# Attention in a layernorm, mixture-of-experts and latent-attention block: the causal mask added on VectorE, one reciprocal per head, one context copy on ScalarE

## The reference, cut to what matters

```python
latents = x @ W_down.T                          # (2, 512, 64)
q, k, v = heads(x @ W_q.T), heads(latents @ W_uk.T), heads(latents @ W_uv.T)
scores = q @ k.T / sqrt(128)
scores = where(causal, scores, -inf)            # a query sees the keys up to itself
attn = softmax(scores, axis=-1)
return (attn @ v) @ W_o.T
```

## Time and profile before

| | |
|---|---|
| time, median of 3 runs | 241.64 us (241.52 to 241.77) |
| the profiled execution | 241.79 us, of which the span of the profile is 240.0 us |
| granted TensorE clock | 1.0 of full speed |
| busy: TensorE / weight loads / VectorE / ScalarE / GpSimd | 97% / 73% / 84% / 69% / 36% |
| instructions | 7215, of which VectorE 480 and ScalarE 320 |
| attention, from the first scores to the end of the last context | 57.0 to 188.8 us of the span |

### The profile page before, as it was taken

How to read it: one execution, slowest core, us unless ns; L and a number is a source line. 1 busy time by engine, 2 the same in 40 slices (tenths; PEclk the granted TensorE clock), 3 DMA queues, 4 the chain that set the end, 5 groups by cost and what they waited for, 6 DMA issues and landing times.

```text
span 240.0 us, 7215 instructions
## 1 busy us (share of the span) xinstructions
PE 232.4 (97%) x2620; PEld 175.4 (73%) x2620; DVE 201.8 (84%) x480; ACT 165.2 (69%) x320; POOL 85.6 (36%) x140
## 2 busy tenths in 40 slices
PE   8799999998999999999999999999999999999995
PEld 2455469846679788787887786887888888864474
DVE  3988789988899999899899999998999547368793
ACT  2667873885788889879798888887988400354660
POOL 8342775090024344345334343543255000300320
PEclk9999999999999999999999999999999999999999
DMA  6999963003021034142160250241504240000005
GB/s 214 242 384 330 203 154 87 4 0 87 3 55 38 3 77 98 32 99 44 44 131 0 66 109 21 73 83 44 116 15 90 44 46 0 3 0 3 0 1 175
DMA packets 43128, 19.30 MB, mean 80 GB/s; under 512 B 33820, under 2 KB 42856, under 8 KB 42856
## 3 DMA queue, kind: packets, MB, share of 16 engines
q1 hardware_dynamic: 41912, 17.91, 31.5%
q10 hardware_dynamic: 1200, 1.18, 1.5%
HBM read 7.55 MB, written 1.05 MB: 36 GB/s over the span
## 4 chain that ended last, share of the span: by engine, by line
PE 81%; DVE 9%; ACT 5%; DMA 2%; issue 1%; SPq 1%; DVEq 0%
PE bank L1172 15%; PE bank L981 12%; PE bank L1253 9%; PE bank L932 8%; PE bank L1162 7%; PE bank L1163 7%; PE bank L1185 4%; PE bank L1186 4%; PE bank L1187 4%; PE bank L1089 3%; PE bank L1164 3%; DMA X<-in_L_attn_x_dram 2%; DVE X L765 1%; PE bank L939 1%; DVE st L656 1%
## 5 line engine op out<-in xcount | busy, mean ns | idle before, releaser
L574 ACT ACTIVATE prob<-bank,nmax 128x384 f32<-128x384 f32 (+3 forms) x128 | 62.3, 527 | 10.8 <-DVE nmax L823 7.6
L832 DVE TENSOR_TENSOR pT_lo<-bank,pT_hi 128x512 f16<-128x512 f32 x80 | 54.7, 683 | 2.6 <-ACT pT_hi L580 1.8
L580 ACT CAST pT_hi<-bank 128x512 f16<-128x512 f32 x80 | 46.8, 586 | 10.2 <-PE bank L1172 9.8
L1172 PE MATMUL bank<-ident,prob 128*128 128x128 f32 x320 | 50.5, 280 | 0.6 <-ACT prob L574 0.6
L430 POOL TENSOR_TENSOR cst<-craw,rsum 128x256 f32<-128x256 f32 x30 | 18.4, 614 | 70.7 <-DVE craw L841 70.7
L1162 PE MATMUL bank<-latT_hi,wqo 128*128 128x384 bf16 (+3 forms) x128 | 38.2, 299 | 0.5 <-DMA wqo<-stage 0.5
L1185 PE MATMUL bank<-lat,pT_hi 128*128 128x65 bf16 x320 | 37.7, 193 | 0.3 <-DVE pT_lo L832 0.3
L1186 PE MATMUL bank<-lat,pT_hi 128*128 128x64 bf16 x320 | 37.9, 195 | 0.0
L1187 PE MATMUL bank<-lat,pT_lo 128*128 128x65 bf16 x320 | 37.5, 192 | 0.0
L1163 PE MATMUL bank<-latT_lo,wqo 128*128 128x384 bf16 (+3 forms) x128 | 36.6, 299 | 0.0
L823 DVE TENSOR_REDUCE nmax<-bank 128x1 f32<-128x512 f32 (+1 forms) x48 | 32.7, 682 | 1.9 <-PE bank L1164 1.9
(11 more groups left out here) (179 smaller groups left out, 466.2 us busy)
## 6 DMA issues: line engine op xcount, KB each, us to landing
wqo<-stage SPq DMA_DIRECT2D x64, 64.0 KB, 2.0
wqo<-in_L_attn_W_o_dram SPq DMA_DIRECT2D x2, 1024.0 KB, 6.5
wqo<-in_L_attn_W_q_dram SPq DMA_DIRECT2D x1, 2048.0 KB, 14.0
out_dram<-X SPq DMA_DIRECT2D x8, 128.0 KB, 1.8
X<-in_L_attn_x_dram ACTq DMA_DIRECT2D x1, 512.0 KB, 7.0
cT<-in_L_attn_W_uk_dram SPq DMA_DIRECT2D x1, 512.0 KB, 15.7
cT<-in_L_attn_W_uv_dram SPq DMA_DIRECT2D x1, 512.0 KB, 11.2
cT<-in_L_ffn_w_dram SPq DMA_DIRECT2D x1, 384.0 KB, 4.9
```

The source lines that it names most:

```text
L574: last = nc.scalar.activation(prob[:, u % 2, cols], bank[SCORE_BANK[u]][:, cols], ACT.Exp, bias=nmax[:, u, n:n + 1])
L580: nc.scalar.copy(pT_hi[:, j % 2, :], bank[3 + j % 2][:, :]).then_inc(pThi_ready, 1)
L832: nc.vector.tensor_tensor(pT_lo[:, j % 2, :], bank[3 + j % 2][:, :], pT_hi[:, j % 2, :], ALU.subtract).then_inc(pTlo_ready, 1)
L1172: last = nc.tensor.transpose(bank[3 + j % 2][:, blk(k)], prob[:, j % 2, blk(k)], ident[:, :])
```

## The change

- **Mask.** The matmul of line 1164 goes. `maskneg` grows from 128 to 512 columns, zero but for the triangle in the last 128. `row_max` becomes one `tensor_tensor_reduce` per piece: it adds the end of `maskneg` that is as wide as the piece to the scores, multiplies by -1, writes the negated masked scores back to their place in PSUM, and takes their minimum into `nmax`. The exponential then reads the scores with a scale of -1. `row_max` also waits for the constants.
- **Contexts and sums.** The copies into `craw` take the column of sums along (4x65 in place of 4x64). VectorE still copies the first sequence's contexts; the second sequence's are copied by ScalarE in a new `take_second_context`, between its exponentials and its split in steps 5 and 10. VectorE's new `invert_sums`, at the end of its own steps 5 and 10, waits for both copies and inverts all eight sums of a head out of SBUF in one instruction. GpSimd's division of either sequence waits for that. The last head of the last pair is handled as before.
- **Loop.** VectorE's loop over the pairs is written out in the program.

```diff
--- before.py
+++ after.py
@@ -56,6 +56,7 @@
     SCALE = 1.0 / float(P) ** 0.5
     EPS = 1e-5
     HUGE = 1.5e38
+    FAR = 3.4e38
 
 
     HEAD_UNITS = [[(0, 2, 0), (0, 0, 3 * P)], [(0, 3, 0)], [(0, 1, 0), (1, 1, 2 * P)],
@@ -90,7 +91,7 @@
         identb = sb("identb", [P, P], BF16)
         tri = sb("tri", [P, P], BF16)
         onesb = sb("onesb", [P, P], BF16)
-        maskneg = sb("maskneg", [P, P], BF16)
+        maskneg = sb("maskneg", [P, SB * P], BF16)
         rank_i = sb("rank_i", [P, NB, E], I32)
         rank = sb("rank", [P, NB, E], F32)
         sel = sb("sel", [P, FC, P], BF16)
@@ -181,7 +182,7 @@
         pT_lo = sb("pT_lo", [P, 2, SEQ], FP16)
         nmax = sb("nmax", [P, UNITS, 2], F32)
         rsum = sb("rsum", [P, B, SB], F32)
-        craw = sb("craw", [P, B, SB, LAT], F32)
+        craw = sb("craw", [P, B, SB, LAT + 1], F32)
         cst = sb("cst", [P, B, SB, LAT], F32)
 
         bank = [ctx.enter_context(nc.psum_tensor(f"bank{i}", [P, 512], F32)) for i in range(8)]
@@ -356,7 +357,7 @@
                                     base=0, pattern=[[-1, P]], channel_multiplier=1)
             nc.gpsimd.affine_select(out=tri[:, :], in_=tri[:, :], compare_op=ALU.is_ge, fill=0.0,
                                     base=0, pattern=[[1, P]], channel_multiplier=-1)
-            nc.gpsimd.affine_select(out=maskneg[:, :], in_=maskneg[:, :], compare_op=ALU.is_ge, fill=-1e30,
+            nc.gpsimd.affine_select(out=maskneg[:, SEQ - P:SEQ], in_=maskneg[:, SEQ - P:SEQ], compare_op=ALU.is_ge, fill=-1e30,
                                     base=0, pattern=[[-1, P]], channel_multiplier=1)
             nc.gpsimd.tensor_copy(rank[:, :, :], rank_i[:, :, :])
             nc.gpsimd.affine_select(out=sel[:, :, :], in_=sel[:, :, :], compare_op=ALU.not_equal, fill=1.0,
@@ -427,7 +428,7 @@
                     of_head = slice(LAT * side, LAT * (side + 1))
                     pool.wait_ge(rsum_ready, i * (2 * B) + (side * B + b + 1))
                     pool.wait_ge(ctx_free, i * (2 * B) + (side * B + B + b + 1))
-                    nc.gpsimd.tensor_tensor(cst[:, b, :, :], craw[:, b, :, :],
+                    nc.gpsimd.tensor_tensor(cst[:, b, :, :], craw[:, b, :, 0:LAT],
                                             rsum[:, b, :].unsqueeze(2).to_broadcast([P, SB, LAT]), ALU.mult).then_inc(cst_ready, 1)
                     pool.wait_ge(cst_ready, i * (2 * B) + (side * B + b + 1))
                     hi, lo = (c[:, bass.ds(i, 1), SB * b:SB * (b + 1), of_head].rearrange("p i n l -> p (i n) l") for c in (c_hi, c_lo))
@@ -572,16 +573,26 @@
                 for n, (b, q, at) in enumerate(HEAD_UNITS[u % HU]):
                     cols = slice(at, at + P * (q + 1))
                     last = nc.scalar.activation(prob[:, u % 2, cols], bank[SCORE_BANK[u]][:, cols], ACT.Exp,
-                                                bias=nmax[:, u, n:n + 1])
+                                                bias=nmax[:, u, n:n + 1], scale=-1.0)
                 last.then_inc(prob_ready, 1)
 
             def split(i, j):
                 act.wait_ge(pT_ps, i * UNITS + (j + 1))
                 nc.scalar.copy(pT_hi[:, j % 2, :], bank[3 + j % 2][:, :]).then_inc(pThi_ready, 1)
 
+            def take_second_context(i, side):
+
+                src = bank[6][:, 0:SB * (LAT + 1)].rearrange("p (q l) -> p q l", q=SB)
+                act.wait_ge(clo_ready, i * (2 * B) + (side * B + B))
+                act.wait_ge(ctx_ps, i * (2 * B) + (side * B + B))
+                nc.scalar.copy(craw[:, 1, :, :], src).then_inc(ctx_free, 1)
+
             def attention_step(i, j, queries=True):
+                side, unit = divmod(j - 1, HU)
                 if not beyond(i, j + 3):
                     exponent(i, j + 3)
+                if j and unit == LAST_UNIT[1]:
+                    take_second_context(i, side)
                 if queries and j in (1, 3):
                     split_queries(i + 1, j // 2)
                 if not beyond(i, j + 2):
@@ -816,15 +827,15 @@
 
             def row_max(i, j):
                 u = j % UNITS
+                dve.wait_ge(const_step, 2)
                 dve.wait_ge(s_ps, i * UNITS + (j + 1))
                 parts = HEAD_UNITS[u % HU]
                 src = bank[SCORE_BANK[u]]
-                if len({q for _, q, _ in parts}) == 1:
-                    last = nc.vector.tensor_reduce(nmax[:, u, 0:len(parts)], src[:, :].rearrange("p (a n) -> p a n", a=len(parts)),
-                                                   AX.X, ALU.max, negate=True)
-                else:
-                    for n, (b, q, at) in enumerate(parts):
-                        last = nc.vector.tensor_reduce(nmax[:, u, n:n + 1], src[:, at:at + P * (q + 1)], AX.X, ALU.max, negate=True)
+                for n, (b, q, at) in enumerate(parts):
+
+                    last = nc.vector.tensor_tensor_reduce(
+                        out=src[:, at:at + P * (q + 1)], in0=src[:, at:at + P * (q + 1)], in1=maskneg[:, SEQ - P * (q + 1):SEQ],
+                        scale=-1.0, scalar=FAR, op0=ALU.add, op1=ALU.min, accum_out=nmax[:, u, n:n + 1])
                 last.then_inc(max_ready, 1)
 
             def split(i, j):
@@ -837,8 +848,12 @@
                 src = bank[5 + b][:, 0:SB * (LAT + 1)].rearrange("p (q l) -> p q l", q=SB)
                 dve.wait_ge(clo_ready, i * (2 * B) + (side * B + 1 + b))
                 dve.wait_ge(ctx_ps, i * (2 * B) + (side * B + b + 1))
-                nc.vector.reciprocal(rsum[:, b, :], src[:, :, LAT]).then_inc(rsum_ready, 1)
-                nc.vector.tensor_copy(craw[:, b, :, :], src[:, :, 0:LAT]).then_inc(ctx_free, 1)
+                nc.vector.tensor_copy(craw[:, b, :, :], src).then_inc(ctx_free, 1)
+
+            def invert_sums(i, side):
+
+                dve.wait_ge(ctx_free, i * (2 * B) + (side * B + 2 * B))
+                nc.vector.reciprocal(rsum[:, :, :], craw[:, :, :, LAT]).then_inc(rsum_ready, B)
 
             def normalise_last(b):
 
@@ -852,14 +867,16 @@
 
             def attention_step(i, j, queries=True):
                 side, unit = divmod(j - 1, HU)
-                if j and unit in LAST_UNIT:
-                    take_context(i, side, LAST_UNIT.index(unit))
+                if j and unit == LAST_UNIT[0]:
+                    take_context(i, side, 0)
                 if not beyond(i, j + 1):
                     split(i, j + 1)
                 if not beyond(i, j + 4):
                     row_max(i, j + 4)
                 if queries and j in (1, 3):
                     split_queries(i + 1, j // 2)
+                if j and unit == LAST_UNIT[-1]:
+                    invert_sums(i, side)
 
             def split_latents(t):
                 dve.wait_ge(lat_hi, t + 1)
@@ -886,7 +903,8 @@
             split(0, 0)
             row_max(0, 3)
             attention_step(0, 0)
-            with dve.Fori(0, NP - 1) as i:
+
+            for i in range(NP - 1):
                 for j in range(1, UNITS + 1):
                     attention_step(i, j)
             for j in range(1, UNITS - 2):
@@ -1160,8 +1178,7 @@
                     keys = slice(SEQ * b, SEQ * b + P * (q + 1))
                     queries_of = uc[:, i * 2 + j // HU, SEQ * b + P * q:SEQ * b + P * (q + 1)]
                     mm(dst[:, cols], queries_of, latT_hi[:, keys], start=True, stop=False)
-                    mm(dst[:, cols], queries_of, latT_lo[:, keys], start=False, stop=False)
-                    last = mm(dst[:, cols][:, P * q:], identb[:, :], maskneg[:, :], start=False, stop=True)
+                    last = mm(dst[:, cols], queries_of, latT_lo[:, keys], start=False, stop=True)
                 last.then_inc(s_ps, 1)
 
             def transposes(i, j):
```

## The result

| | before | after |
|---|---|---|
| median | 241.62 us (4 runs) | 243.38 us (4 runs) |
| ratio | | 1.0065, 95% interval 1.0042 to 1.0087 |
| span of the profiled execution | 240.0 us | 241.6 us |
| one trip of the loop (100.50 to 116.80 after) | 16.22 us | 16.30 us |
| end of the last context | 188.8 us | 190.4 us |

Behind the last context both kernels take the same time (240.0 - 188.8 and 241.6 - 190.4, both 51.2). The 1.6 us are lost in attention, and I place them by where TensorE begins the first query product of each pair (before: 63.30, 79.64 and 160.72; after: 63.62, 80.23 and 161.64) and its last context (188.62 and 190.23): 0.3 until the first, 0.3 in the first trip, 0.3 over the next five, 0.7 behind 160.72 and 161.64.

The account below looks back on a forecast made before the run. The bound was to go from TensorE to VectorE: a trip of 15.5 + 0.15 = 15.6 us instead of 16.22, 0.6 x 7.7 trips = 4.7 us less, median 237.0 us. Range 234.4 to 243; the forecast's own 236.4 to 239.5.

Parts of the forecast that it names:

- TensorE's 0.88 us a trip: Attention loop: removing 16 mask matmuls at 0.055 us each shortens TensorE's trip from 16.22 to 15.34 us.
- a: VectorE's new mask-and-minimum pass: extra cost per pass beyond a pass of the kind already traced, taken as 0.07 us.
- Rivals 3 and 4: VectorE's new pass: result waits for drain, 249.5 us, chance 0.12; reading and writing one PSUM bank halves it, 278, chance 0.06.
- rival 1: Attention loop: VectorE follows easily, TensorE keeps the pace at 15.34 us a trip, total 235.0 us; chance 0.28.
- so TensorE sets the pace and VectorE has less than 0.8 us to spare: Attention loop before: TensorE busy for all 16.22 us of a trip, VectorE for 15.45.
- The copy on ScalarE ... which hides it: Steps with ScalarE's context copy: split and VectorE's subtraction come 0.36 us later twice a trip, hidden by TensorE's two-unit delay.
- 0.15 a trip: VectorE's waits in the attention loop, allowed for the inversion and an occasionally late pT_hi, in us.
- the 0.3 at an inversion: Sign of being wrong: VectorE waits more than 0.3 us at an inversion of the sums.
- over 16: Sign of being wrong: a trip of the attention loop takes more than 16 us.
- Covered: GpSimd's two divisions in a row take 4.2 us; the first takes 2.1, due three units later (about 4 us).
- The loop, the memset, the wait on the constants: VectorE's written-out loop, GpSimd's wider maskneg memset (0.2 to 0.4 us) and the extra wait: no gain or cost expected.
- Rival 2: Attention loop: gain eaten by a near 0.10 or VectorE waiting 0.3 to 0.4 us per inversion; 241.1 us, chance 0.12.

Follow-up runs that it names:

- light_split: Kernel before without mask matmuls (not causal), VectorE's subtraction for the low part of the probabilities over 256 of 512 columns: 234.84 us, ratio 0.9716.
- no_mask: Kernel before with the mask matmuls of line 1164 left out and nothing in their place (not causal): 239.47 us, ratio 0.9902.
- no_mask_short: Kernel before without mask matmuls (not causal), query products of steps 1 and 3 cut from six matmuls to four: 233.90 us, ratio 0.9663.
- short_queries: Changed kernel with the query products of steps 1 and 3 cut from six matmuls to four (less exact): 239.84 us, ratio 0.9908.
- by_phase: Kernel before, mask on VectorE only in units 5, 6, 7: old contexts, loop written out, 240.12 us; or second context copied late by ScalarE, separate reciprocals, 239.80.
- mask_only: Changed kernel with both sequences' contexts and their reciprocals on VectorE as before the change: 242.35 us, ratio 1.0039 to the kernel before.
- late_invert: Changed kernel with VectorE's inversion moved behind its subtraction of the next step: 248.73 us, ratio 1.0294 to the kernel before.
- late_both: Changed kernel with VectorE's inversion behind its next subtraction and ScalarE's context copy behind its split: 246.16 us, ratio 1.0189 to the kernel before.
- unroll_only: Kernel before with only VectorE's loop over the pairs written out: 241.60 us, ratio 0.9994.

## Why the prediction was wrong

- **TensorE's 0.88 us a trip**: right. The trip is 15.34 in light_split.
- **The new pass**: a was taken as 0.07 and is 0.01 to 0.03 (0.61 against 0.60; 0.72 against 0.67 for two). VectorE's issued work came to 14.9 us a trip, not 15.5. Rivals 3 and 4 fall with it: the next pass doesn't wait for the read, and writing the bank that is read costs next to nothing. With the right a the prediction's two sums would have given rival 1's 235.0, further from the 243.4 than the forecast: this size is not what failed. (At 15.65 for the trip the sum itself gives about 237.3; its own range, by the same sum, is 236.8 to 239.9 and not 236.4 to 239.5.)
- **The step that failed: "so TensorE sets the pace and VectorE has less than 0.8 us to spare", and from it a trip as the larger of two sums.** VectorE's spare time lies in the steps with queries, where TensorE has 1.3 us more to do and VectorE can't work ahead, since it has no scores yet. Without the two query products of 1.29 us each TensorE's trip is 13.6, or 1.36 a unit. VectorE's ten subtractions, its maxima and contexts are 6.0 + 6.28 + 1.6 by the earlier trace rows, or 1.39 a unit: in those steps it was already as slow. The waits hinted at it: ten waits for scores in five trips, two a trip, as many as there are query products. I averaged them over the trip. A trip is the sum over its phases of the slower engine, as long as no third one holds that engine up. no_mask shows it (0.28 of 0.88, as much as the five matmuls of steps 1 to 3 take, 5 x 0.055), no_mask_short and short_queries show where TensorE's time counts, the two by_phase kernels show where the mask's does. This explains the gain that didn't come; the loss of 1.7 us comes with the next point, in the trips, and at the two ends of attention.
- **"The copy on ScalarE ... which hides it"**: wrong. I asked when TensorE needs `pT_lo`, two units later, and not when VectorE needs `pT_hi`: at once, as VectorE has no slack in these steps. ScalarE's copy cost less than I took (0.26, not 0.36), and VectorE's hole was 0.59 us from 122.57 to 123.16, 0.1 of it the reciprocal, where I had allowed 0.15 a trip. That is over the 0.3 at an inversion that was named as a sign of being wrong, and so is the trip of 16.30, over 16. mask_only, without that copy, has trips of 16.2 again.
- **"Covered" for GpSimd**: right for the changed kernel, but the margin is 0.5 us and not the 2 I gave it. The prediction's "three units later (about 4 us)" was miscounted: from the inversion at the end of step 5 to the copy that opens step 8 lie two steps, 2.6 us (123.11 to 125.70), and the division takes 2.1. late_invert and late_both show how near that edge is.
- **The loop, the memset, the wait on the constants**: right. unroll_only shows it for the loop; the wider memset can have cost no more than 0.07 us, by which TensorE's first query product came later (49.07 against 49.00); the wait on the constants shows in no row.
- **Rival 2** (the gain is eaten) was the nearest, at 241.1 with 0.12; I let it decide by a or by waits at the inversion. The waits came, a did not; but the rival still took all that TensorE saves as won first, which it never was. Slower than before had 0.21.

The 0.7 us of mask_only, which has neither the copy on ScalarE nor the late inversion, lie at the ends. By its profile, against the kernel before, it loses 0.2 us between TensorE's query products at 49.00 (50.29 in mask_only) and VectorE's first subtraction, wins 0.1 over the seven trips, and loses 0.4 in the last pair. (Its profiled execution had also lost 1.3 us before attention, at a clock of 0.97 over the first 50 us; the median doesn't have that.) Why the last pair costs more with the mask on VectorE stays open: no run varies it by itself, and in the changed kernel it is 0.6 of the 1.7 us. Spreading the query products over more steps, which would lessen the phases instead of using them, wasn't tried.

## What to carry to other kernels

An engine that is busy for all of a loop's time can still be shadowed by another that is nearly as busy: before you add up a period, cut it into the stretches that lie between the other engine's waits, give each stretch to its slower engine, and ask which third engine that one would wait for next. Work moved onto an engine belongs in the stretches in which that engine waits; elsewhere the same move brings nothing or costs. And when results are merged to save an instruction, look for whoever is served later by it, on every engine (here GpSimd), and at the margin it has left.

## What the runs showed of the hardware

A VectorE pass that adds an SBUF tile to PSUM, writes back in place to the same bank and keeps a running minimum holds the engine 0.61 us for 512 columns, nearly as long as a plain maximum or a subtraction (0.60). A pair of 384 and 128 columns takes 0.72 against 0.67. Its accumulator read shows a row of 0.14 us that starts together with the next pass.
